# A recommender with cross layers on one core: weights laid out by the host, early rows of the first squares, and a later transpose of the second group

## Chip, cores and metric

One core of a Trainium2 chip runs the whole program. The metric is the device time of one execution in microseconds, the median of several runs. The profile shown is of one execution.

## The reference

39 embedding tables are looked up for a batch of 2048 rows, which gives `e` of (2048, 39, 16). Three cross layers follow (`w0` of 39x39x128, `w1` and `w2` of 39x64x128), then a sum over the 16 channels, the dense context, and three dense layers.

```python
x0 = xk = e                                             # (2048, 39, 16)
for idx, (W, b) in enumerate(((w0, b0), (w1, b1), (w2, b2))):
    z = relu(einsum('bhd,bkd,hks->bsd', x0, xk, W) + b[None, :, None])    # (2048, 128, 16)
    if idx < 2:
        xk = z[:, :64, :]; direct.append(z[:, 64:, :])
    else:
        direct.append(z)
z = sum(concatenate(direct, axis=1), axis=-1)           # (2048, 256)
h = concatenate([z, dense_ctx], axis=1)                 # (2048, 272)
h = maximum(h @ W_top1 + b_top1, 0); h = maximum(h @ W_top2 + b_top2, 0)
y = h @ W_top3
```

## The kernel before

**Groups, turns and tiles.** The batch is cut into 16 groups of 128 rows, and each group into two chunks of 8 channels, 1024 columns (`COLS`) each. A chunk is a turn, 32 in all (turn 0 to 31). A turn has 47 tiles: PAIRED, 0 to 19, cross layer 1 (each tile holds two fields h times 64 maps, 128 partitions); SQUARED, 20 to 26, cross layer 0 of the *next* chunk (three shifted copies of the 39 fields, 117 partitions; the last has 78); and LAST, 27 to 46, cross layer 2. Turn -1 has squares alone. Per tile VectorE multiplies two operands into a slot of `prod`, and TensorE contracts it over the partitions into PSUM (`zacc`). `PLAN` (line 58) gives each tile a letter: F tiles are contracted in float32 with `w_plain`; V, D and P tiles are split in a rounded `high` part (made by ScalarE) and a `low` part (VectorE for V and D, GpSimd for P), and contracted by three cheaper passes with `w_high` and `w_low`.

**Engines.** Each engine has its own stream, written by a function `emit(turn, j)` that `turns` calls for each turn and tile in order, the middle turns in a hardware loop. The streams meet in semaphores. An instruction that waits holds up everything behind it on its engine.

**Data.** x of a group is gathered by GpSimd (39 indirect DMAs into `landed`, line 602), transposed by TensorE in five blocks of 128 rows (the last has 112) into `maps2`, copied to `x` by ScalarE, and written twice in a row to DRAM (`x_periods`) by SP. From there SP loads `spread` (each field repeated over 64 partitions, two DMAs per piece of two tiles, ten pieces; line 510), `x_thrice` (three shifted copies of the 39 fields, line 500) and `shifted` (a ring of 4 slots, three DMAs of 39 rows of 4 KB per tile of squares, line 490). A slot of the ring is loaded again when the product that read it is done. In steady state the 20 spread loads of the next turn are issued during LAST, each after the product that frees its piece.

**The start.** Group 0 is gathered, turned and written block by block (`write_block`, line 521). w1 and w2 are loaded in four DMAs, and w0 in 50 short runs of a diagonal from SP and nearly as many from ScalarE's queue (lines 465 and 669), into space at the end of `spread`. ScalarE then copies tiles one by one into `w_plain`, `w_high` and PSUM (`cast_weights`), and VectorE subtracts for `w_low`. On SP, block q's write is followed, for q below 3, by a wait until it has landed and by the loads of two pieces of `spread`; blocks 3 and 4 follow without loads. Then `load_first` waits for all five blocks and loads x_thrice and four squares whole (`shifted` 0 to 3). The remaining four pieces of `spread` wait for the prepared weights (`s_prep`).

**The second group.** GpSimd copies its indices (`numbers`), issues 12 gathers at once, two per square of turn -1, and 13 in tiles 0 to 12 of turn 0. TensorE transposes it behind tile 13 of turn 0 (`TURN_AT`), ScalarE copies at 15, SP writes at 16, and from tile 20 (`GATHER_AT`) GpSimd gathers the next group.

**The end.** In turn 31 SP loads the top layers' weights and the dense context when tile 34's product is done (`load_top`, ten DMAs), ScalarE casts them behind tile 41, TensorE transposes the context in two halves (`turn_dense`, line 1073: behind tile 42 and after LAST), and VectorE makes the low parts of the first features and of the context (lines 972 and 965) after the last tile's low part. Then TensorE runs `MLP_STEPS`.

## Time and profile before

| | us |
|---|---|
| three timed runs, median (lowest to highest) | 2534.72 (2532.46 to 2537.24) |
| the profiled execution, its own time | 2519.62 |
| its span | 2517.8 |
| TensorE busy in the span | 2404.7 (96%) |
| VectorE busy | 2247.7 (89%) |
| GpSimd busy | 1687.2 (67%) |
| ScalarE busy | 1070.0 (42%) |
| mean granted clock of TensorE, share of full speed | 0.994 |

The span is the time between the first and last instruction of the profiled execution. Times in a timeline count from its start. The DMA share is the mean busy share of the core's 16 DMA engines; it can come out slightly over 1.

### The profile page before, as it was taken

What the parts mean: (1) busy time and instruction counts of PE and PEld (TensorE: products, weight loads), DVE (VectorE), ACT (ScalarE), POOL (GpSimd) and SP (SyncE); (2) the same over time, 40 slices, a digit from 0 to 9 for tenths busy, and PEclk for the clock granted to TensorE, in tenths of its full rate; (3) what the DMA queues carried; (4) which work ended last, traced back from release to release, by engine and by line L of the source; (5) the groups of instructions that cost most, each with busy time, mean ns of one, the idle gap of its engine ahead of it and who ended that gap; (6) DMA issues with size and microseconds to landing.
All of it is one profiled execution on the core that took longest, in us unless ns stands there. A gap on an engine that the chain in (4) does not pass through costs nothing.

```text
span 2517.8 us, 30358 instructions
## 1 busy us (share of the span) xinstructions
PE 2404.7 (96%) x7734; PEld 1447.4 (57%) x7734; DVE 2247.7 (89%) x1686; ACT 1070.0 (42%) x1124; POOL 1687.2 (67%) x1062
## 2 busy tenths in 40 slices
PE   0589999999999999999999999999999999999999
PEld 0355565555556665655566565556665565665556
DVE  0579999999999999999999999999999997999983
ACT  2234434444443444444344444444444443444445
POOL 6767676776767677776767677676768777544340
PEclk9999999999999999999999999999999999999999
DMA  7868889888888988888899888888998886998820
GB/s 151 189 142 192 193 194 213 197 191 199 192 198 194 221 195 195 199 190 200 191 207 205 195 197 193 200 191 197 217 198 201 191 199 159 211 203 194 188 70 11
DMA packets 184402, 469.77 MB, mean 187 GB/s; under 512 B 37842, under 2 KB 74307, under 8 KB 184371
## 3 DMA queue, kind: packets, MB, share of 16 engines
q1 hardware_dynamic: 161181, 461.92, 79.8%
q0 software_dynamic: 19968, 5.15, 2.0%
q10 hardware_dynamic: 3223, 2.35, 0.4%
q8 instruction: 13, 0.21, 0.0%
q14 instruction: 17, 0.14, 0.0%
HBM read 456.96 MB, written 12.33 MB: 186 GB/s over the span
## 4 chain that ended last, share of the span: by engine, by line
PE 73%; POOL 13%; issue 8%; DVE 2%; DMA 2%; SPq 2%; ACT 1%; POOLq 0%; DVEq 0%; ACTq 0%
PE zacc_a L1014 30%; PE zacc_b L1014 29%; POOL low L624 7%; POOL landed L602 6%; PE zacc_a L1049 5%; PE zacc_b L1049 5%; DMA x_periods<-x 1%; SPq L465 1%; DVE prod L908 1%; DMA shifted<-x_periods 1%; POOL mark L608 1%; PE zacc_a L1046 0%; PE zacc_b L1046 0%; ACT high L788 0%; PE maps L1056 0%
## 5 line engine op out<-in xcount | busy, mean ns | idle before, releaser
L624 POOL TENSOR_TENSOR low<-prod,high 128x1024 fp32r<-128x1024 f32 x384 | 945.8, 2472 | 579.8 <-ACT high L788 576.2
L908 DVE TENSOR_TENSOR prod<-spread,maps 128x2048 f32<-128x2048 f32 x448 | 1017.2, 2282 | 89.5 <-ACT direct L735 29.7
L788 ACT ACTIVATE high<-prod 128x1024 fp32r<-128x1024 f32 (+1 forms) x576 | 595.9, 1056 | 710.9 <-DVE prod L908 444.3
L602 POOL DMA_INDIRECT landed<-in_tbl,rows_id x624 | 672.4, 1078 | 179.2 <-issue 160.8
L1014 PE MATMUL zacc_a<-prod,w_plain 128*128 128x512 f32 (+2 forms) x1536 | 710.7, 597 | 30.0 <-DVE prod L893 24.1
L1014 PE MATMUL zacc_b<-prod,w_plain 128*128 128x512 f32 (+2 forms) x1536 | 705.3, 593 | 5.9 <-DVE prod L908 5.9
L1014 PEld LDWEIGHTS zacc_a<-prod,w_plain 128*128 128x128 f32 (+2 forms) x1536 | 292.5, 191 | 303.2 <-issue 271.2
L1014 PEld LDWEIGHTS zacc_b<-prod,w_plain 128*128 128x128 f32 (+2 forms) x1536 | 290.7, 189 | 274.3 <-issue 246.6
L893 DVE TENSOR_TENSOR prod<-shifted,x_thrice 117x1024 f32<-117x1024 f32 (+1 forms) x224 | 265.8, 1222 | 70.6 <-DMA shifted<-x_periods 53.3
L1049 PE MATMUL zacc_b<-low,w_high 128*128 128x512 f32 x672 | 280.4, 498 | 8.6 <-POOL low L624 8.6
L1049 PE MATMUL zacc_a<-low,w_high 128*128 128x512 f32 x672 | 280.3, 498 | 2.0 <-POOL low L624 2.0
L912 DVE TENSOR_TENSOR prod<-spread,maps 128x1024 f32<-128x1024 f32 (+1 forms) x224 | 265.6, 1210 | 0.0
L1014 PE MATMUL zacc_a<-high,w_low 128*128 128x512 f32 x672 | 239.0, 437 | 0.0
L1014 PE MATMUL zacc_b<-high,w_low 128*128 128x512 f32 x672 | 237.4, 434 | 1.5 <-ACT high L788 1.4
L1014 PE MATMUL zacc_a<-high,w_high 128*128 128x512 f32 x672 | 211.7, 396 | 0.0
L1014 PE MATMUL zacc_b<-high,w_high 128*128 128x512 f32 x672 | 211.3, 396 | 0.0
L1049 PEld LDWEIGHTS zacc_b<-low,w_high 128*128 128x128 f32 x672 | 126.8, 190 | 108.5 <-issue 82.8
L1049 PEld LDWEIGHTS zacc_a<-low,w_high 128*128 128x128 f32 x672 | 126.9, 189 | 101.3 <-issue 77.3
L865 DVE TENSOR_TENSOR low<-prod,high 128x1024 fp32r<-128x1024 f32 x128 | 165.0, 1289 | 0.0
L1014 PEld LDWEIGHTS zacc_b<-high,w_low 128*128 128x128 f32 x672 | 126.3, 189 | 58.3 <-issue 30.5
L1014 PEld LDWEIGHTS zacc_a<-high,w_low 128*128 128x128 f32 x672 | 126.1, 189 | 53.7 <-issue 30.7
L1014 PEld LDWEIGHTS zacc_a<-high,w_high 128*128 128x128 f32 x672 | 127.1, 189 | 29.9
(117 smaller groups left out, 1608.8 us busy)
## 6 DMA issues: line engine op xcount, KB each, us to landing
spread<-x_periods SPq DMA_DIRECT2D x608, 512.0 KB, 14.9
shifted<-x_periods SPq DMA_DIRECT2D x640, 156.0 KB
x_thrice<-x_periods SPq DMA_DIRECT2D x96, 156.0 KB
landed<-in_tbl,rows_id POOLq DMA_INDIRECT x624, 6.3
spread<-x_periods SPq DMA_DIRECT2D x32, 256.0 KB, 20.3
x_periods<-x SPq DMA_DIRECT2D x30, 256.0 KB, 3.6
spread<-features SPq DMA_DIRECT2D x4, 512.0 KB, 4.6
features<-feat ACTq DMA_DIRECT2D x15, 128.0 KB, 6.3
```

Of the source, the lines that this page charges most:

```text
L465: sp.dma_start(st0a[s * FIELDS + lo:s * FIELDS + hi, u, :], w0_run(f * FIELDS + g, hi - lo)).then_inc(s_wload, 16)
L602: nc.gpsimd.indirect_dma_start(out=landed[:, f, :], out_offset=None, in_=tables[f], in_offset=bass.IndirectOffsetOnAxis(ap=rows_id[:, f:f ...
L608: nc.gpsimd.tensor_tensor(mark[:, 0:1], mark[:, 0:1], mark[:, 1:2], ALU.add).then_inc(s_mark, 1)
L624: nc.gpsimd.tensor_tensor(low[0:rows, at_, :], prod[0:rows, at_, :], high[0:rows, slot(j, SPLIT, NH), :], ALU.subtract).then_inc(s_lowp, 1)
L788: nc.scalar.activation(high[0:rows, h, :], made(turn, j)[0:rows, :], ACT.Copy).then_inc(s_round, 1)
L865: nc.vector.tensor_tensor(to, whole, top, ALU.subtract).then_inc(s_lowv, 1)
L893: nc.vector.tensor_tensor(to, shifted[0:rows, u % RING0, :], x_thrice[0:rows, :], ALU.mult).then_inc(s_square, 1)
L908: nc.vector.tensor_tensor(prod[:, at_:at_ + 2, :], spread[:, t:t + 2, :], maps[:, :].unsqueeze(1).to_broadcast([128, 2, COLS]), ALU.mult). ...
L912: nc.vector.tensor_tensor(to, spread[0:rows, t, :], maps[0:rows, :], ALU.mult).then_inc(s_prod, 1)
L1014: return nc.tensor.matmul(z[:, hf * BANK:(hf + 1) * BANK], w, x[:, hf * BANK:(hf + 1) * BANK], start=start, stop=stop)
L1049: done = nc.tensor.matmul(z[:, cols], w_high[0:rows, r, :], x[:, cols], start=False, stop=last)
```

## The change

- The host lays out all weights (`laid_out`): w_plain and w_parted in the order of their slots, w0 as two tensors of 117 rows (`w0_ab`, `w0_ba`), biases and small vectors packed, the context already transposed (`dense_t`). They are loaded whole by SP: the plain tiles straight into `w_plain`, the parted ones into `prod`. ScalarE makes `w_high` in one instruction and VectorE sums the two halves of w0 and subtracts for `w_low`, one instruction each.
- SP, after block 3 has landed, loads the *early* rows (fields 0 to 31) of x_thrice and of squares 0 to 3; block 4 is then written, waited for, and the *late* rows (32 to 38) of x_thrice and square 0 are loaded from SP, those of squares 1 to 3 from ScalarE's queue.
- Group 1's gathers read `all_ids` directly, 20 ahead and one in each of tiles 0 to 18 of turn 0; each waits only for the transposes of the block it overwrites. Its transposes go behind tile 26 (into `maps1`), the copy to 27, the write to 28, and the third group's gathers begin behind tile 27.
- In turn 31 SP loads context and `W_top1`'s last rows at tile 0 into the free `shifted` and `x_thrice`; ScalarE casts them at tiles 6 to 16, GpSimd clears the gaps at tile 0, VectorE makes their low parts at tile 20. W_top1 and W_top2 are loaded behind tile 30's product and cast at tiles 36 and 39, the first features' casts move to tile 45, and their low part to tile 0 of turn 32. The context's transposes on TensorE are gone.

```diff
+TURN0_AT, COPY0_AT, WRITE0_AT, GATHER0_AT = 26, 27, 28, 27
+GATHERED_AHEAD = 20
-TOP_TILES, FEATS_TILES = 8, 12
-CAST_AT, TURN_TOP_AT = 41, 42
+TOP_TILES, FEATS_TILES, FH_TILES = 4, 8, 12
+CTX_AT = (6, 8, 12, 14, 16)
+CAST_AT, W1L_AT, FEATS_AT = (36, 39), 38, 45
...
+        def square_rows(u, late):
+
+            if late:
+                return [(FIRST_FIELDS - PER0 * u, FIELDS - PER0 * u)]
+            return [run for run in ((0, FIRST_FIELDS - PER0 * u), (FIELDS - PER0 * u, FIELDS)) if run[0] < run[1]]
+
+        def thrice_rows(s, late):
+
+            if late:
+                return [run for run in ((0, s), (FIRST_FIELDS + s, FIELDS)) if run[0] < run[1]]
+            return [(s, FIRST_FIELDS + s)]
+
+        FIRST_FIELDS = len(BLOCKS[0]) * (TURNED - 1)
...
+        def chunk0(first, rows):
+
+            flat = x_periods[0, :, :, :].rearrange("k (f d) b -> (k f) (d b)", d=DIM)
+            return flat[first:first + rows, 0:COLS]
+
+        def load_thrice0(engine, late):
+
+            for s in range(PER0):
+                for lo, hi in thrice_rows(s, late):
+                    engine.dma_start(x_thrice[s * FIELDS + lo:s * FIELDS + hi, :], chunk0(FIELDS - s + lo, hi - lo)
+                                     ).then_inc(s_thrice, 16)
+
+        def load_shifted0(engine, u, late):
+
+            for s in range(PER0):
+                for lo, hi in square_rows(u, late):
+                    engine.dma_start(shifted[s * FIELDS + lo:s * FIELDS + hi, u, :], chunk0(PER0 * u + lo, hi - lo)
+                                     ).then_inc(s_shifted[u], 16)
...
+            sp.dma_start(parts_in[:, 0:plan_r - PARTED0, :], a["w_parted"]).then_inc(s_parts, 16)
+            sp.dma_start(w_plain[0:TRIPLE, plan_f - PLAIN0:plan_f, :], a["w0_ab"][:, 0:PLAIN0, :]).then_inc(s_w0, 16)
+            sp.dma_start(w0_other, a["w0_ba"]).then_inc(s_w0, 16)
...
+            sp.dma_start(w_plain[:, 0:plan_f - PLAIN0, :], a["w_plain"]).then_inc(s_plain, 16)
+            sp.dma_start(bias[:, :], a["bias"]).then_inc(s_const, 16)
+            sp.dma_start(small[:, :], a["small"]).then_inc(s_const, 16)
...
-            third = -(-len(W0_RUNS) // EARLY_BLOCKS)
             for q in range(TURNED):
-                load_w0(W0_RUNS[third * q:third * (q + 1)])
                 write_block(q)
+                sp.wait_ge(s_first_w, 16 * PERIODS * (q + 1))
                 if q < EARLY_BLOCKS:
-                    sp.wait_ge(s_first_w, 16 * PERIODS * (q + 1))
                     for piece in (2 * q, 2 * q + 1):
                         load_spread(Turn(None, 0), piece)
+                elif q < TURNED - 1:
+                    load_thrice0(sp, 0)
+                    for u in range(RING0):
+                        load_shifted0(sp, u, 0)
+                else:
+                    load_thrice0(sp, 1)
+                    load_shifted0(sp, 0, 1)
+
+            def load_context():
+
+                sp.wait_ge(s_square, CHUNKS * N0)
+                sp.dma_start(m_dense, a["dense_t"]).then_inc(s_dense, 16)
+                sp.dma_start(m_w1d, a["w_top1d"]).then_inc(s_dense, 16)
...
                 if turn.fixed and turn.number() == CHUNKS - 1:
+                    if j == 0:
+                        load_context()
...
+            def cast_context(step):
+
+                if step == 0:
+                    act.wait_ge(s_dense, 32)
+                    act.wait_ge(s_gaps, 1)
+                if step < 4:
+                    at_, cols = 32 * (step % 2), slice(step // 2 * COLS, (step // 2 + 1) * COLS)
+                    nc.scalar.activation(m_ctx[at_:at_ + DENSE, cols], m_dense[:, cols], ACT.Copy).then_inc(s_dense_c, 1)
+                    return
...
-                if turn.fixed and turn.number() == CHUNKS - 1 and j == CAST_AT:
-                    cast_top()
-                if turn.fixed and turn.number() == CHUNKS and j == 0:
-                    high_features(0)
-                    copy_dense(0)
+                if turn.fixed and turn.number() == CHUNKS - 1:
+                    if j in CTX_AT:
+                        cast_context(CTX_AT.index(j))
+                    if j in CAST_AT:
+                        cast_top(CAST_AT.index(j))
+                    if j == FEATS_AT:
+                        high_features(0)
...
-                if turn.fixed and turn.number() == CHUNKS and j == SUB:
-                    split_top()
+                if turn.fixed and turn.number() == CHUNKS - 1 and j == SQUARED[0]:
+                    low_context()
+                if turn.fixed and turn.number() == CHUNKS and j == 0:
+                    low_features(0)
...
                 if turn.fixed and turn.number() == -1 and j == 0:
-                    pe.wait_ge(s_const, 16 * 4)
+                    pe.wait_ge(s_const, 16 * CONSTS)
                     turn_first()
...
-                if j == TURN_AT and not turn.odd and turn.shift(2).real():
+                if j == (TURN0_AT if turn.fixed and turn.number() == 0 else TURN_AT) and not turn.odd and turn.shift(2).real():
                     turn_x(turn.shift(2))
```

## Rows read from the trace of the kernel before

**Rows 1.** The page: busy time of each engine.

```profile
PE 2404.7 (96%) x7734; PEld 1447.4 (57%) x7734; DVE 2247.7 (89%) x1686; ACT 1070.0 (42%) x1124; POOL 1687.2 (67%) x1062
```

**Rows 2.** Stretches: length, each engine's busy time (instructions), PEclk, DMA share, GB/s.

```profile
103.00:145.60 42.60, 35.76 (x104) 21.50 (x104) 31.83 (x20) 11.89 (x13) 30.94 (x22) 0.86 0.47 126
145.60:217.95 72.35, 72.35 (x232) 43.41 (x231) 66.71 (x50) 31.29 (x30) 54.08 (x34) 1.00 0.82 184
```

**Rows 3.** Timeline of VectorE, the start (start us, us, what, idle before).

```profile
79.69 1.23 DVE L893 TENSOR_TENSOR prod<-shifted,x_thrice 117x1024 f32<-117x1024 f32 x1 [14.58 <-DMA shifted<-x_periods]
...
93.73 1.22 DVE L893 TENSOR_TENSOR prod<-shifted,x_thrice 78x1024 f32<-78x1024 f32 x1 [0.57 <-DMA shifted<-x_periods]
```

**Rows 4.** Timelines of TensorE and VectorE between LAST and the top layers.

```profile
2455.76 1.92 PE L1073 MATMUL maps<-spread 128*16 128x128 f32 x16
2459.31 0.47 PE L1134 MATMUL zacc_a<-spread_r 80*128 80x512 f32 x1 [1.63 <-issue]
...
2457.99 1.22 DVE L965 TENSOR_TENSOR spread_r<-maps,spread_r 16x1024 fp32r<-16x1024 f32 x1
```

**Rows 5.** Timeline of SP: loads issued.

```profile
58.27 2.58 SPq L510 DMA_DIRECT2D spread<-x_periods  x4
...
71.45 1.15 SPq L500 DMA_DIRECT2D x_thrice<-x_periods  x3
...
2351.50 28.97 SPq L510 DMA_DIRECT2D spread<-x_periods  x20
```

**Rows 6.** DMA issues at 58.3, 60.2, 61.3, 20.8 and 2380: KB, us to landing.

```profile
spread<-x_periods SPq DMA_DIRECT2D x1, 512.0 KB, 4.9
...
spread<-x_periods SPq DMA_DIRECT2D x2, 512.0 KB, 9.3
...
x_periods<-x SPq DMA_DIRECT2D x2, 64.0 KB, 9.2
...
x_periods<-x SPq DMA_DIRECT2D x1, 64.0 KB, 2.1
...
spread<-x_periods SPq DMA_DIRECT2D x1, 256.0 KB, 20.4
```

**Rows 7.** Stretches: spreads alone, 39-row loads, their last two engines, after w0 loads.

```profile
48.00:49.00 1.00, 0.00 (x0) 0.00 (x0) 0.00 (x0) 0.00 (x0) 0.85 (x1) 1.00 0.99 205
209.00:210.00 1.00, 1.00 (x6) 0.79 (x5) 1.00 (x1) 0.00 (x0) 0.69 (x2) 1.00 0.86 246
215.00:215.25 0.25, 0.25 (x2) 0.21 (x2) 0.25 (x1) 0.25 (x1) 0.25 (x1) 1.00 0.13 51
55.75:56.00 0.25, 0.00 (x0) 0.00 (x0) 0.00 (x0) 0.00 (x0) 0.00 (x0) 1.00 0.10 18
```

**Rows 8.** Timeline of TensorE, the transposes of x.

```profile
18.15 0.45 PE L1056 MATMUL maps<-ident,landed 128*128 128x128 f32 x1 [18.15 <-DMA landed<-in_tbl,rows_id]
...
39.90 0.48 PE L1056 MATMUL maps<-ident,landed 128*128 128x128 f32 x1 [12.88 <-DMA landed<-in_tbl,rows_id]
...
134.11 0.59 PE L1083 MATMUL maps<-ident 128*128 128x2 f32 x2 [4.80 <-DMA landed<-in_tbl,rows_id]
```

**Rows 9.** Timeline of GpSimd in turn 0.

```profile
122.67 0.95 POOL L602 DMA_INDIRECT landed<-in_tbl,rows_id  x1 [0.30 <-issue]
...
126.14 2.37 POOL L624 TENSOR_TENSOR low<-prod,high 128x1024 fp32r<-128x1024 f32 x1
128.68 1.77 POOL L602 DMA_INDIRECT landed<-in_tbl,rows_id  x1 [0.16 <-issue]
```

**Rows 10.** Turn 31: timelines of ScalarE and TensorE, then the chain, loop and LAST.

```profile
2390.93 1.06 ACT L788 ACTIVATE high<-prod 128x1024 fp32r<-128x1024 f32 x1 [1.32 <-DVE prod L908]
...
2394.02 0.62 PE L1014 MATMUL zacc_b<-high,w_low 128*128 128x512 f32 x2
...
2281.32 6.07 PE zacc_b L1014 x16
...
2420.44 8.91 PE zacc_b L1014 x16
```

More of the change, by code:

```diff
@@ L221, in build @@
         mark = sb("mark", [128, 2])
-        mark_dve = sb("mark_dve", [128, 2])
+        small = sb("small", [128, 8])
         rows_id = sb("rows_id", [ROWS, FIELDS], i32)
@@ L429, in build, with turned_in @@
-        early_tiles = [j for j in [*PAIRED, *LAST] if j not in later_split]
-        late_tiles = [*SQUARED, *later_split]
-        def weight_home(j):
-            tiles = early_tiles if j in early_tiles else late_tiles
-            r = [i for i in tiles if PLAN[i] != "F"].index(j)
-            return [*zacc, maps1][r // 8][:, r % 8 * MAPS:(r % 8 + 1) * MAPS]
+        def turned_in(n):
+            return maps1 if n.fixed and n.number() == 2 else maps2
         def first_bank(q):
             return q % 2 * BANK
-        def w0_run(start, n):
-            return w0.rearrange("h k s -> (h k) s")[start:start + (n - 1) * (FIELDS + 1) + 1:FIELDS + 1, :]
+        def square_rows(u, late):
+            if late:
+                return [(FIRST_FIELDS - PER0 * u, FIELDS - PER0 * u)]
+            return [run for run in ((0, FIRST_FIELDS - PER0 * u), (FIELDS - PER0 * u, FIELDS)) if run[0] < run[1]]
@@ L556, in emit @@
                 nxt, after = turn.shift(1), turn.shift(2)
-                if turn.fixed and turn.number() == -1 and j == 0:
-                    load_first(nxt)
-                if j == WRITE_AT and not turn.odd and after.real():
+                if j == (WRITE0_AT if turn.fixed and turn.number() == 0 else WRITE_AT) and not turn.odd and after.real():
                     write_x(after)
@@ L598, in _, with gather @@
             nc.gpsimd.memset(mark[:, :], 0.0).then_inc(s_mark, 1)
-            def gather(first, last, of=None):
+            def gather(first, last, of=None, rows=rows_id):
                 for f in range(first, last):
@@ L725, in take @@
                         act.wait_ge(s_sum01, turn.count(1, 1))
+                    if turn.fixed and turn.number() == 0:
+                        act.wait_ge(s_x, 2)
                     to, keep, s = maps1, HALF, s_z0
@@ L789, in emit @@
                                          ).then_inc(s_round, 1)
-                if j == COPY_AT and not turn.odd and turn.shift(2).real():
+                if j == (COPY0_AT if turn.fixed and turn.number() == 0 else COPY_AT) and not turn.odd and turn.shift(2).real():
                     copy_x(turn.shift(2))
@@ L1174, with laid_out, take, tile @@
-W0_RUNS = w0_runs()
-N_WLOADS = 2 * len(W0_RUNS) - sum(u == s == 0 for u, s, _, _ in W0_RUNS)
+def laid_out(given):
+    def take(name, dtype=np.float32):
+        return np.asarray(given.pop(name), dtype)
+    w0, flat = take("L0_rec_w0"), {1: take("L0_rec_w1").reshape(-1, MAPS), 2: take("L0_rec_w2").reshape(-1, MAPS)}
+    def tile(j):
+        t = j if j in PAIRED else j - LAST[0]
+        rows = flat[layer_of(j)][128 * t:128 * t + rows_of(j)]
+        return np.concatenate([rows, rows]) if stacked(j) else rows
+    ab, ba = np.zeros((TRIPLE, N0, MAPS), np.float32), np.zeros((TRIPLE, N0, MAPS), np.float32)
+    for n, j in enumerate(SQUARED_ORDER):
+        u, i = j - N1, np.arange(FIELDS)
+        for s in range(rows_of(j) // FIELDS):
+            f, g = (i - s) % FIELDS, (i + PER0 * u) % FIELDS
+            ab[s * FIELDS:(s + 1) * FIELDS, n] = w0[f, g]
+            if (u, s) != (0, 0):
+                ba[s * FIELDS:(s + 1) * FIELDS, n] = w0[g, f]
+    given["w0_ab"], given["w0_ba"] = ab, ba
+    for name, tiles in (("w_plain", PLAIN), ("w_parted", PARTED)):
+        given[name] = np.ascontiguousarray(np.stack([tile(j) for j in tiles if j not in SQUARED], axis=1))
+    given["bias"] = np.stack([take(b) for b in ("L0_rec_b0", "L0_rec_b1", "L0_rec_b2")], axis=1)
+    wt1, wt2 = take("W_top1"), take("W_top2")
+    given["w_top1"] = np.stack([np.concatenate([wt1[HALF:MAPS], wt1[:HALF]]), wt1[MAPS:2 * MAPS]], axis=1)
+    given["w_top1d"] = np.ascontiguousarray(wt1[2 * MAPS:])
+    given["w_top2"] = np.ascontiguousarray(wt2.reshape(4, 128, D3).transpose(1, 0, 2))
+    given["small"] = np.concatenate([take("W_top3").reshape(2, 128).T, take("b_top1").reshape(4, 128).T,
+                                     take("b_top2").reshape(2, 128).T], axis=1)
+    given["dense_t"] = np.ascontiguousarray(take("dense_ctx").T)
+    given["ident"] = np.eye(128, dtype=np.float32)
+    return given
```

304 lines of the change are left out of this document (120 added, 184 removed).

## The prediction

> **What bounds the kernel now.** I began with the page: TensorE is busy for 2404.7 of 2517.8 us and VectorE for 2247.7 [rows 1], so only time in which TensorE stands still, or does work that can go, can be won. Next, the stretches between one turn's squares and the next: inside the loop TensorE is busy for the whole of 72.35 us, at full clock [rows 2]. Nothing in the change touches that loop. What is open lies at the two ends, and I read those by the timelines of single engines. The first product of squares runs at 79.69 and the seventh at 93.73 [rows 3]; turn 0 then takes 42.60 us from its first PAIRED matmul (103.0) to the squares (145.6), with TensorE busy 35.76 of it and the clock granted at 0.86 [rows 2]. At the far end TensorE finishes LAST, transposes the context for 1.92 us, and starts the top layers at 2459.31 [rows 4]; from there it hardly pauses.
>
> **The start, step by step.** Today's chain on SP is: write a block of x, wait until it has landed, load four spreads; block 2's spreads are issued from 58.27 [rows 5]. One such step has a fixed length: of four spreads issued from 58.27 the first lands after 4.9 us and the last, issued at 60.2, after 9.3, at 69.5; the two writes issued behind them take 9.2 us although each has only 64 KB, where a write that follows nothing takes 2.1 [rows 6]. So transfers of one queue are served in order, and a write behind four spreads lands 12.2 us after the first spread's issue.
>
> The changed chain. The casts on ScalarE and the 50 narrow loads of w0 on each side go, but bias and small are now issued behind the weights, some 3.46 MB (23 parted and 17 plain tiles of 64 KB, twice 0.42 MB of squares), issued from 3.2 us. At about 220 GB/s, the rate of such stretches (205 and 246 in two of them [rows 7]), they are in near 21 us, and TensorE, which waits for all constants before its first transpose, starts near 21 instead of 18.15 [rows 8]. Copy and issue take 1 us, the write 2.1 alone and more behind the last weights: block 0 lands at about 25, with bounds at 23.5 and 27. Then 12.2 us to 37.2; block 2 is gathered only at 39.9 [rows 8], so its write goes out at 40.5 but lands behind the spreads at 49.5; 12.2 more, and block 3 has landed at 61.7. Now SP issues 24 loads of early rows, 15 times 128 KB. How they are dealt over the 16 DMA engines decides the case.
>
> What the rows show: 39-row loads keep the DMA share at 0.86 where spreads of 64 partitions keep 0.99, and yet move more, 246 against 205 GB/s [rows 7]. 0.86 is near 13 of 16, and 13 is the largest divisor of 39 up to 16. So I read: a transfer runs on as many engines as divide its rows. Early rows come in runs of 32, 26, 29, 23 and small ones; 29 and 23 have no divisor above 1, so all their rows go through one engine, 3 x 29 + 3 x 23 rows, and with its share of the others 183 rows of 4 KB, 750 KB, on the first engine, against 12 to 27 rows on the rest. Dealt evenly (3 rows per engine also gives 13 for 39) it would be 30. The trace has one hint more: the narrow loads of w0, runs such as 25, 23 and 21 rows, leave a tail in which 0.10 of the engines work, at 18 GB/s [rows 7]. I take the one-engine reading.
>
> The Trainium skill, DMA: Bandwidth & Descriptors, section Why a DMA increments its semaphore by 16 and not by 1, states that rule: the largest number up to 16 that divides the slowest dimension, the lowest engines first, 127 partitions all on one. The trace agrees for 39 rows, and no run here shows 29. By the rule the time is the forecast; by even dealing it would be the first rival's.
>
> Price: a lone engine. When two engines are left at work, 51 GB/s move [rows 7], 24.5 each, 0.17 us a row; in company 246/13 = 18.9, 0.22 us a row. 9 us in company take 41 rows, the other 142 take 24.2: 33.2 us, bounds 31 (all lone) and 40 (all in company), and 9 if dealt evenly. Block 4's write uses all engines and stands behind that: 61.7 + 2.6 + 33.2 + 1.1 = 98.6. Then 8 late loads on SP at 0.38 us (1.15 for three [rows 5]) and 2.1 to land: first product at 103.7, not 79.69. The first four then run back to back, the last three wait for their loads (each needs a slot that a product frees, some 4.7 us from there, 2.2 between two): the seventh ends 10.9 us after the first starts, at 114.6. Now it ends at 94.95 (93.73 [rows 3] and 1.22). **Cost +19.6 us** (+14 to +29); dealt evenly, 9 in place of 33.2 gives **-4**. Folding and splitting the weights, 7 and 23 tiles of 128 columns at the 1.23 us per 1024 of a product [rows 3], make 4.5 us on VectorE from 58 on, and the cast on ScalarE is earlier: all under this wait.
>
> **Turn 0.** TensorE no longer waits at tile 13 for the second group's gathers: 4.80 us now [rows 8], plus the transposes and a slow clock after it. What is late next is GpSimd: 20 gathers are ahead instead of 26, so six stand between its low parts of tiles 11 and 17, not two. Tile 11's ends at 128.5; the next gather comes at 128.68 and takes 1.77, a quiet one 0.95, with 0.30 before each [rows 9]. Two slow and four quiet ones reach 137.8, the low part of 2.4 us ends at 140.2, and the squares start at 140.7 instead of 145.6: **-4.9** (-6.4 to -2). The transposes come back behind tile 26, **+0.7**. SP's write of group 1 now waits for them, and turn 1's spreads, queued behind that wait on SP, start some 6 us later relative to the turn. The DMA share in turn 1 is 0.82 [rows 2], so it is mostly absorbed; **+1.0** (0 to 3). GpSimd's denser gathers of the third group fit in the idle time before its low parts; at one or two places within a us.
>
> **The end.** A new wait: in turn 31 SP issues the context loads at tile 0, when the last spreads have just been issued (2351.50 + 28.97 [rows 5]), and these take 20.4 us to land [rows 6]. The context is behind them in the same queue: in near 2402. ScalarE waits for it behind tile 6, with the casts of tile 7 and after queued behind. That cast runs at 2390.93 now, and TensorE takes tile 7 at 2394.02 [rows 10]. New: 2402.2, one context cast of 1.05, tile 7's of 1.06: 2404.3. TensorE stands for 10.3 us. After the pause before LAST its first 16 matmuls took 8.91 us where they take 6.07 in the loop [rows 10], so 2.8 more: **+13.1** (+10 to +15). VectorE's low_context (3 us at tile 20) then fits beneath. Casts of W1 and W2 move to tiles where ScalarE idles, with W1's low part on GpSimd.
>
> Against it: both context transposes go, 1.92 us each [rows 4], and what stands between LAST and the top layers: the context's low part and low_features, the last ending at 2459.2 [rows 4]. low_features now comes before tile 46's low part; that ends near 2452.7 and TensorE starts the top near 2454.0: **-5.3** (-6.5 to -4).
>
> **Sum**: 19.6 - 4.9 + 0.7 + 1.0 + 13.1 - 5.3 = +24.2 us, on the profiled execution's 2519.6 us (span and 1.8 around it), that is 2543.8 there. The three timed runs have a median of 2534.7, 15.1 above the profiled one; both ends are unlikely to change that, so 2534.7 + 24.2 = 2558.9.
>
> **The rivals.** First, early rows dealt evenly, the rest as above: +24.2 - 23.6 = +0.6, 2535.3, no change. For: 3 rows on 13 engines fits 0.86 too; against: the tail of few engines. 0.14. Second, a faster outcome: even dealing, and the context is not behind the spreads (small rows overtaking): 13.1 becomes 0.7 for low_context in a gap that it does not quite fit, so 2534.7 - 11.8 = 2522.9; against: the 64 KB write that took 9.2 us. 0.07. Third, one engine for the early rows, but no wait for the context: 2546.5. 0.12. Fourth, worse: turn 1's DMA backlog does not drain and the early loads go at 18.9 GB/s: 2570. 0.07. It decides from a backlog of about 6 us on, the slack between the last spread's landing and its product.
>
> **Numbers.** The forecast has 0.60. Its own range is 2550 to 2568. With the third rival inside, 0.72 is held; reaching to the first takes it to 0.86, so 2533 to 2568. One case in a few will be off in its own size. Faster or slower by 0.2% is 5.1 us, about what a measurement of this kernel tells from nothing: faster 0.09 (the second and part of the first), same 0.13, slower 0.78.
>
> **What would show it.** In the new profile: one SP stretch of 24 loads near 62 us followed by 20 to 30 us with a DMA share near 0.06 and about 24 GB/s; first product of squares near 104; no wait of TensorE on gathers at tile 13, a short one on GpSimd near tile 19; in turn 31 a wait of about 10 us on ScalarE's cast at tile 7; top layers starting at once behind LAST. If the share stays near 0.9 after the early loads and the first product comes near 80, the dealing was even and the forecast is wrong by 24 us; if tile 7 is not late, the order of the queue was misread, and 12 us go.

## The result and the profile after

The changed kernel takes 2553.0 us (median of 4 runs, 2551.7 to 2558.0) beside 2534.9 for the kernel before on the same chip: ratio 1.0075, 95% interval 1.0062 to 1.0087, 18 us slower. The forecast was 2559, with a range of 2533 to 2568 and 0.78 for slower. The number came near, but the sum behind it did not hold as written: one term was absent on this chip, and others that I had not seen or had put too low stood in its place.

One fact is needed to read any of it. The kernel before does not take the same time on all chips: 2535.7 and 2535.5 us on two chips of the experiments, 2516.4 and 2518.2 on two others. Its shown profile (2519.6) is of the quick kind, the times of the study of the slow kind. This is the start of the kernel before on a chip where it takes 2516, SP's timeline (start us, us, what) and VectorE's first and seventh product of squares:

```profile
15.74 5.74 SPq L465 DMA_DIRECT2D spread<-in_L_rec_w  x17
...
28.99 6.87 SPq L465 DMA_DIRECT2D spread<-in_L_rec_w  x17
...
79.45 1.22 DVE L893 TENSOR_TENSOR prod<-shifted,x_thrice 117x1024 f32<-117x1024 f32 x1 [13.44 <-DMA shifted<-x_periods]
...
93.57 1.22 DVE L893 TENSOR_TENSOR prod<-shifted,x_thrice 78x1024 f32<-78x1024 f32 x1 [0.72 <-DMA shifted<-x_periods]
```

And the same kernel where it takes 2535:

```profile
15.84 13.94 SPq L465 DMA_DIRECT2D spread<-in_L_rec_w  x17
...
39.94 18.23 SPq L465 DMA_DIRECT2D spread<-in_L_rec_w  x17
...
98.63 1.22 DVE L893 TENSOR_TENSOR prod<-shifted,x_thrice 117x1024 f32<-117x1024 f32 x1 [14.77 <-issue]
...
112.81 1.22 DVE L893 TENSOR_TENSOR prod<-shifted,x_thrice 78x1024 f32<-78x1024 f32 x1 [0.98 <-DMA shifted<-x_periods]
```

Seventeen narrow loads of w0 take SP 5.74 us on one chip and 13.94 on the other, the next seventeen 6.87 and 18.23. On the slow kind nearly all of SP's issues stand 0.70, 1.40 or 2.1 us apart between 18 and 58 us, where those of w0 stand 0.3 to 0.4 apart on the quick kind. I call SP *stepped* there. It steps once more from 92 to 108 us, beside the second group's gathers:

```profile
91.27 17.58 SPq L490 DMA_DIRECT2D shifted<-x_periods  x20
```

These 20 loads take 12.33 us on the quick kind. That costs the start nothing: from the first to the seventh product are 14.1 us on the quick chip and 14.2 on the slow one. The changed kernel was profiled on a chip of the slow kind, and it steps too, in another place. Its SP timeline, one issue alone, and VectorE's first and seventh product:

```profile
59.81 1.27 SPq L464 DMA_DIRECT2D x_thrice<-x_periods  x3
61.12 27.56 SPq L471 DMA_DIRECT2D shifted<-x_periods  x21
88.68 0.70 SPq L542 DMA_DIRECT2D x_periods<-x  x2
...
76.08 0.70 SPq L471 DMA_DIRECT2D shifted<-x_periods  x1
...
99.11 4.63 DVE L896 TENSOR_TENSOR prod<-shifted,x_thrice 117x1024 f32<-117x1024 f32 x4 [36.09 <-DMA shifted<-x_periods]
...
109.14 1.22 DVE L896 TENSOR_TENSOR prod<-shifted,x_thrice 78x1024 f32<-78x1024 f32 x1 [1.13 <-DMA shifted<-x_periods]
```

And two stretches of it (length, busy time of PE, PEld, DVE, ACT and POOL, PEclk, DMA share, GB/s):

```profile
64.00:72.00 8.00, 0.00 (x0) 0.00 (x0) 0.00 (x0) 0.00 (x0) 6.02 (x7) 1.00 0.22 48
...
84.00:92.00 8.00, 0.00 (x0) 0.00 (x0) 0.00 (x0) 0.00 (x0) 0.00 (x0) 1.00 0.14 46
```

The 21 early loads of squares take 27.56 us to issue while the DMA engines are used at a share of 0.22, then 0.14: up to 89.4 it is SP that binds, not the engines. Behind that, block 4's write takes until 93.9 to land.

Turn 0 and turn 1, TensorE: the first PAIRED matmuls of turn 0, the squares of turn 0 and of turn 1, and the two long waits:

```profile
120.42 3.75 PE L1011 MATMUL zacc_a<-prod,w_plain 128*128 128x512 f32 x4 [5.86 <-DVE prod L911]
...
159.16 1.22 PE L1046 MATMUL zacc_a<-low,w_high 128*128 128x512 f32 x2 [4.50 <-POOL low L643]
160.18 6.13 PE L1011 MATMUL zacc_b<-prod,w_plain 117*128 117x512 f32 x8
...
218.57 1.22 PE L1046 MATMUL zacc_b<-low,w_high 128*128 128x512 f32 x2 [6.23 <-DVE low L866]
...
244.91 3.60 PE L1011 MATMUL zacc_a<-prod,w_plain 117*128 117x512 f32 x8
```

[rows 2] has 103.0, 145.6 and 217.95 for the three. Turn 0 is 39.76 us in place of 42.60 (43.4 in the two other traces of the kernel before). The 4.80 us on the gathers [rows 8] are gone and 4.50 on GpSimd's low part of tile 17 have come; behind that wait the squares begin at half clock, the 1.2 GHz level (granted 0.56 of full speed from 160.2 to 166.0; eight matmuls in 6.13 us, 3.60 at full clock). Turn 1 is 84.73 us in place of 72.35 [rows 2]. Its long wait is on a low part of VectorE:

```profile
207.15 1.22 DVE L866 TENSOR_TENSOR high<-prod,high 64x1024 fp32r<-64x1024 f32 x1
...
210.60 7.92 DVE L866 TENSOR_TENSOR low<-prod,high 128x1024 fp32r<-128x1024 f32 x1
...
204.82 0.96 POOL L621 DMA_INDIRECT landed<-in_tbl,rows_id  x1 [0.16 <-issue]
...
207.34 1.85 POOL L621 DMA_INDIRECT landed<-in_tbl,rows_id  x1 [0.31 <-issue]
209.49 0.95 POOL L621 DMA_INDIRECT landed<-in_tbl,rows_id  x1 [0.30 <-issue]
210.46 6.96 POOL L643 TENSOR_TENSOR low<-prod,high 128x1024 fp32r<-128x1024 f32 x3
```

A subtraction of as many columns (on 64 partitions) takes 1.22 us at 207.15, the one at 210.60 takes 7.92, and over that time GpSimd runs three low parts with nothing between them, from 210.46 to 217.42.

The end: SP's loads, then ScalarE and TensorE in turn 31, the first matmuls of LAST (2460.53), and the first of the top layers:

```profile
2379.14 28.61 SPq L531 DMA_DIRECT2D spread<-x_periods  x20
2407.80 0.59 SPq L561 DMA_DIRECT2D shifted<-in_dense_t  x1
...
2429.95 1.06 ACT L764 ACTIVATE shifted_r<-shifted 16x1024 fp32r<-16x1024 f32 x1 [13.35 <-DMA x_thrice<-in_w_top1d]
...
2432.00 1.22 PE L1011 MATMUL zacc_b<-high,w_low 128*128 128x512 f32 x2 [10.84 <-ACT high L798]
...
2460.53 3.75 PE L1011 MATMUL zacc_b<-prod,w_plain 128*128 128x512 f32 x4 [5.89 <-DVE prod L911]
...
2495.15 0.73 PE L1043 MATMUL zacc_b<-high,w_low 128*128 128x512 f32 x2 [1.55 <-DVE high L866]
...
2496.19 0.40 PE L1121 MATMUL zacc_a<-shifted_r,x_thrice_r 80*128 80x512 f32 x1
...
2497.13 0.63 PE L1125 MATMUL zacc_a<-spread_r 128*128 128x512 f32 x1
```

The context loads leave SP behind the last 20 spreads and land 21 us after their issue; ScalarE stands 13.35 us and TensorE 10.84, close to the 10.3 forecast.

Put against a trace of the kernel before on the same kind of chip, stretch by stretch (us; a turn from the first matmul of PAIRED to the squares, or from squares to squares):

| | before, quick chip | before, slow chip | after (slow chip) | after less before, slow |
|---|---|---|---|---|
| start, to the first PAIRED matmul | 102.86 | 122.10 | 120.42 | -1.7 |
| turn 0, to its squares | 43.37 | 43.45 | 39.76 | -3.7 |
| to turn 1's squares | 72.31 | 72.34 | 84.73 | +12.4 |
| rest | 2298.3 | 2298.2 | 2311.3 | +13.1 |
| span | 2516.8 | 2536.1 | 2556.2 | +20.1 |

The profiled execution of the changed kernel is 5 us above its other three; the medians differ by 18. The two columns of before differ in the start alone. The rest, +13.1, is not all at the end: +1.7 lies in turns 2 to 30 (1.5 of it from the squares of turn 3 to those of turn 4, 77.36 us in place of 75.85; its cause is open), and +11.35 from turn 30's squares (2367.72, before 2359.00) to the end.

### The profile page after: what moved, and what is told of

It is laid out like the page before. It is cut to its first block, busy times and chain, and to the rows that moved or that the text cites. A ratio compares the mean times of both kernels' runs of the same rounds, so it can differ in the third digit from the quotient of the medians.

```text
span 2556.2 us, 30130 instructions
## 1 busy us (share of the span) xinstructions
PE 2407.8 (94%) x7702; PEld 1448.5 (57%) x7702; DVE 2251.4 (88%) x1657; ACT 1058.5 (41%) x1053; POOL 1689.2 (66%) x1059
## 3 DMA queue, kind: packets, MB, share of 16 engines
HBM read 457.02 MB, written 12.33 MB: 184 GB/s over the span
## 4 chain that ended last, share of the span: by engine, by line
PE 67%; POOL 12%; issue 8%; DVE 3%; DMA 1%; ACT 0%; POOLq 0%; SPq 0%; ACTq 0%; DVEq 0%
PE zacc_a L1011 28%; PE zacc_b L1011 26%; POOL low L643 6%; POOL landed L621 5%; PE zacc_a L1046 5%; PE zacc_b L1046 5%; DMA x_thrice<-in_w_top1d 1%; DVE prod L911 1%; DVE low L866 1%; POOL mark L627 1%; PE zacc_b L1043 0%; PE zacc_a L1043 0%; DVE zacc_a L915 0%; DVE prod L915 0%; PE maps L1053 0%
## 5 line engine op out<-in xcount | busy, mean ns | idle before, releaser
L621 POOL DMA_INDIRECT landed<-in_tbl,rows_id x585 | 631.3, 1079 | 166.4 <-issue 150.8
L866 DVE TENSOR_TENSOR low<-prod,high 128x1024 fp32r<-128x1024 f32 x128 | 171.7, 1341 | 0.0
L1011 PEld LDWEIGHTS zacc_b<-high,w_high 128*128 128x128 f32 x672 | 127.8, 190 | 30.1
```

The source lines that it names most:

```text
L621: nc.gpsimd.indirect_dma_start(out=landed[:, f, :], out_offset=None, in_=tables[f], in_offset=bass.IndirectOffsetOnAxis(ap=rows[:, f:f + 1 ...
L866: nc.vector.tensor_tensor(to, whole, top, ALU.subtract).then_inc(s_lowv, 1)
L1011: return nc.tensor.matmul(z[:, hf * BANK:(hf + 1) * BANK], w, x[:, hf * BANK:(hf + 1) * BANK], start=start, stop=stop)
```

## The experiments

All ratios are to the kernel before on the same chip; what its time there was is said, since it tells the kind of chip.

**e1_even: the early rows dealt evenly.**

```diff
-            return [run for run in ((0, FIRST_FIELDS - PER0 * u), (FIELDS - PER0 * u, FIELDS)) if run[0] < run[1]]
+            n = FIRST_FIELDS - PER0 * u
+            cuts = (0, n) if n in (32, 26) else (0, 16, n) if n == 29 else (0, 13, n)
+            return [*zip(cuts, cuts[1:]), *([(FIELDS - PER0 * u, FIELDS)] if u else [])]
```

> The changed kernel with the early rows of squares 1 and 3 cut differently: 29 rows as 16 + 13, 23 rows as 13 + 10, the same rows to the same places, 6 loads more. One-engine reading: the most loaded DMA engine then carries some 33 rows in place of 183; the 27.56 us of issuing shrink to about 9, the last block has landed near 77 instead of 93.9, the first product of squares comes near 83 instead of 99.1, and the time falls by 15 us (12 to 18), to 1.001 of the kernel before. Rival, that the loads were slow beside the second group's gathers, however they are dealt: the issuing stays at 27 us or more, first product at 99 or later, ratio 1.0075 or a little above.

Measured: ratio 1.0065 (1.0052 to 1.0079), before 2535.7. The expected 15 us did not come; the first product is at 98.2. SP's timeline:

```profile
61.48 29.23 SPq L473 DMA_DIRECT2D shifted<-x_periods  x27
90.76 0.80 SPq L544 DMA_DIRECT2D x_periods<-x  x2
92.83 1.49 SPq L466 DMA_DIRECT2D x_thrice<-x_periods  x5
```

27 loads take 29.23 us, again stepped: cutting a load in two gives the engines less each and SP more to issue. What did change is the tail. Block 4's write leaves SP at 90.8 to 91.6 and has landed at 92.8; in the changed kernel it leaves at 88.7 and lands at 93.9, at a DMA share near one engine in 16. So the write lands 5.2 us after it leaves SP with the uneven dealing and 2.0 with the even one: the uneven dealing is there, but most of it is hidden by SP on this chip. The median, 2553.2 beside 2553.0, does not move, and the test does not tell what the dealing costs where SP does not step.

**e2_ctx: the context loads ahead of the last spreads.**

```diff
-                    if j == 0:
-                        load_context()
+                if turn.fixed and turn.number() == CHUNKS - 2 and j == LAST[0]:
+                    load_context()
```

> The changed kernel with the two context loads issued one turn earlier, ahead of the last turn's spreads instead of behind them. Queue reading: the 10.8 us in which TensorE stood for ScalarE's cast of tile 7 in turn 31 go, and the slow clock behind them (about 2 us): 10 to 13 us less than the changed kernel, ratio 1.0025. Cost bounded at 1 us: the spreads leave SP a little later. Rival, that the loads are slow by themselves or that something else holds ScalarE there: the wait stays, ratio 1.0075.

Measured: ratio 1.0026 (1.0017 to 1.0035), before 2535.7: 12.4 us less than 1.0075, as expected. The loads, from the DMA issues around them (KB each, median us to landing):

```profile
shifted<-in_dense_t SPq DMA_DIRECT2D x1, 128.0 KB, 2.7
```

TensorE at the end, timeline:

```profile
2448.92 3.75 PE L1011 MATMUL zacc_b<-prod,w_plain 128*128 128x512 f32 x4 [5.89 <-DVE prod L911]
...
2483.51 0.73 PE L1043 MATMUL zacc_b<-high,w_low 128*128 128x512 f32 x2 [1.54 <-DVE high L866]
...
2484.54 0.40 PE L1121 MATMUL zacc_a<-shifted_r,x_thrice_r 80*128 80x512 f32 x1
```

Issued first they land in 2.7 us, and TensorE's 10.84 us wait is gone: their place behind the spreads in the queue was the cause. LAST to top layers is 35.62 us (2448.92 to 2484.54), 35.66 in the changed kernel (2460.53 to 2496.19); before it was 38.87 [rows 4, 10]. Here the top layers run at full clock from their first matmul.

**e4_whole: no early rows; block 4 is written at once, then 15 whole loads.**

```diff
-                elif q < TURNED - 1:
-                    load_thrice0(sp, 0)
-                    for u in range(RING0):
-                        load_shifted0(sp, u, 0)
-                else:
-                    load_thrice0(sp, 1)
-                    load_shifted0(sp, 0, 1)
+                elif q == TURNED - 1:
+                    load_first(Turn(None, 0))
```

(and the late loads on ScalarE's queue go)

> The changed kernel without early rows: block 4 is written as soon as it is copied, and then the 15 whole loads of 39 rows are issued as in the kernel before. If the early rows only stood in the way: block 4 is issued near 60, has landed near 62.5, and as in the kernel before 8.2 us lie between the first of these loads and the first product of squares, so near 71 in place of 99.1, 28 us earlier. GpSimd still has 20 gathers to issue and may give 5 of it back in turn 0. 23 to 28 us less than the changed kernel, ratio 0.9965 (0.995 to 0.9985). Rival, that the DMA engines are held by the gathers in this stretch so that whole loads are slow too: first product near 90 or later, ratio 1.004 or more.

Measured: ratio 0.9998 (0.9986 to 1.0011), before 2535.7. That is some 19 us less than the changed kernel, and less than the 23 to 28 expected. So on this kind of chip the early rows cost 19 us over not having them. The first product is where I put it, the seventh is not:

```profile
63.20 3.50 SPq L520 DMA_DIRECT2D x_thrice<-x_periods  x3
67.40 23.13 SPq L510 DMA_DIRECT2D shifted<-x_periods  x20
...
70.13 1.23 DVE L887 TENSOR_TENSOR prod<-shifted,x_thrice 117x1024 f32<-117x1024 f32 x1 [6.93 <-DMA shifted<-x_periods]
...
93.32 1.22 DVE L887 TENSOR_TENSOR prod<-shifted,x_thrice 78x1024 f32<-78x1024 f32 x1 [1.17 <-DMA shifted<-x_periods]
```

20 loads of 39 rows take 23.13 us here, 13.75 in the shown trace of the kernel before (SP's timeline, from 72.64), and PAIRED starts at 102.61. Whole loads step as early ones do, and until about the same time.

**e5_old2: the second group at its old places.**

```diff
-TURN0_AT, COPY0_AT, WRITE0_AT, GATHER0_AT = 26, 27, 28, 27
-GATHERED_AHEAD = 20
+TURN0_AT, COPY0_AT, WRITE0_AT, GATHER0_AT = 13, 15, 16, 20
+GATHERED_AHEAD = 26
```

(and the group's transposes into `maps2`, as before)

> The changed kernel with the second group back at its old places: 26 gathers ahead, turned behind tile 13, the third group's gathers from tile 20. Theory: turn 0 gets its wait of some 4.8 us at tile 13 back (+3), and turn 1 loses its 6 us wait behind tile 46's neighbours, the slow clock after it and the transposes (84.7 back to about 74): 7 to 9 us less than the changed kernel in all, ratio 1.0042. Rival, that turn 1 is late from the DMA work that the slow start pushed into it: turn 1 stays near 84, turn 0 gets 3 longer, ratio 1.0085.

Measured: ratio 1.0045 (1.0031 to 1.0058), before 2535.7: 7.6 us less. PAIRED starts at 121.93, squares at 164.06 and 236.37: turn 0 gives back 2.4 us and turn 1 is 72.31 again, 12.4 less. The placement of the second and third groups' work was the whole of turn 1's loss. The 7.6 us here and the 12.4 of e2_ctx make 20.0, as much as the whole loss; the two edits were not run together with the early rows.

**e9_calm: no gathers just before GpSimd's three low parts in a row.**

```diff
-def gather_slots(behind):
+def gather_slots(behind, none=()):
...
-    free = [p for p in range(behind + 1, 2 * TILES) if PLAN[p % TILES] != "P"]
+    free = [p for p in range(behind + 1, 2 * TILES) if PLAN[p % TILES] != "P" and p not in none]
...
-GATHERS, GATHERS0 = gather_slots(GATHER_AT), gather_slots(GATHER0_AT)
+GATHERS, GATHERS0 = gather_slots(GATHER_AT), gather_slots(GATHER0_AT, range(44, 53))
```

> The changed kernel, but none of the third group's gathers stands at places 44 to 52, before and among GpSimd's three low parts in a row at the start of turn 1 (tiles 3, 4, 5); they are spread over the other places. Theory: these gathers made GpSimd late, its three low parts ran back to back, and VectorE's low part beside them took 7.92 instead of 1.22 us; without them VectorE's takes 1.2 to 3 us, TensorE's wait of 6.2 us and the slow clock behind it go, turn 1 takes 84 instead of 92.2 from first product to first product: 7 to 9 us less than the changed kernel, ratio 1.0043. Rival: turn 1 is late because the group is turned behind tile 26 and its spreads come later; then the 92.2 stay, ratio 1.0075.

Measured: ratio 1.0128 (1.0111 to 1.0145), but before takes 2516.4 here, so the ratio does not stand beside 1.0075; the trace does:

```profile
209.72 1.22 DVE L866 TENSOR_TENSOR low<-prod,high 128x1024 fp32r<-128x1024 f32 x1
...
207.40 2.41 POOL L643 TENSOR_TENSOR low<-prod,high 128x1024 fp32r<-128x1024 f32 x1 [2.05 <-ACT high L798]
211.88 4.75 POOL L643 TENSOR_TENSOR low<-prod,high 128x1024 fp32r<-128x1024 f32 x2 [2.07 <-ACT high L798]
```

VectorE's low part takes 1.22 us, TensorE's wait of 6.2 us is gone, and turn 1 is 75.72 us (squares at 160.57 and 236.29) instead of 84.73: 9.0 us. The group is still turned behind tile 26. So most of turn 1's loss comes from where the third group's gathers stand. The other 3.4 us were not taken apart; the transposes and a half clock behind turn 0's wait (eight matmuls in 4.90 us) lie in them.

By the whole time the gain is smaller. Turn 2 takes 76.40 us here and 74.64 in the changed kernel, so 1.8 of the 9.0 come back. The median is 2549.3 us (2545.9 to 2551.6), 3.7 below the changed kernel's 2553.0 on another chip, where 7 to 9 were expected. The cleaner pair is e11_even and e1_even, which differ by this edit alone and ran on chips of one kind: 2547.1 beside 2553.2, 6.1 us.

This trace also shows the start on a chip where SP does not step, SP's timeline and two stretches:

```profile
60.80 18.77 SPq L471 DMA_DIRECT2D shifted<-x_periods  x21
79.62 1.25 SPq L542 DMA_DIRECT2D x_periods<-x  x2
93.26 1.49 SPq L464 DMA_DIRECT2D x_thrice<-x_periods  x5
```

```profile
72.00:80.00 8.00, 0.00 (x0) 0.00 (x0) 0.00 (x0) 0.00 (x0) 5.97 (x7) 1.00 0.16 35
84.00:92.00 8.00, 0.00 (x0) 0.00 (x0) 0.00 (x0) 0.00 (x0) 0.00 (x0) 1.00 0.06 26
```

SP has issued all 24 early loads and the write behind them by 80.9 (five of the loads take it 1.2 to 3.8 us each). The gathers end at 82.3. From 84 to 92 nothing else is under way and the share is 0.06 at 26 GB/s, one engine of 16, until block 4 lands at 93.3. This is the stretch that I had forecast (a share near 0.06 and about 24 GB/s), though it stands alone for 9 us and not for the 20 to 30 forecast. PAIRED starts at 120.94, against 102.86 for the kernel before on this chip: +18.1.

**e11_even: e9 with even early rows.** The edit is that of e1_even on top of e9_calm.

> The version without gathers at places 44 to 52, with the early rows of squares 1 and 3 dealt as 16 + 13 and 13 + 10. Where SP issues at its normal pace nothing hides the one engine: that version then had its first product at 98.8 and a stretch of one engine in 16 (share 0.06, 25 to 27 GB/s) up to 92. One-engine reading: with even pieces block 4 is written near 72, the first product comes near 82, and the time is 14 to 17 us less, ratio 1.007 in place of 1.0128. Rival: early rows are slow for another reason, first product near 98 again, ratio 1.013. If SP is in its slow state on this chip, first product near 98 in any case, ratio 1.004.

Measured: ratio 1.0045 (1.0031 to 1.0059), before 2535.5: SP stepped again (27 loads in 29.18 us, first product at 97.8), the case that the expectation names last. So no run has even pieces on a chip where SP does not step, and what the dealing costs there is untested.

**e6_before and e12_before: the kernel before again.**

> The kernel before, unchanged, for a second trace of it. Its timed runs lie 15 us above the one profiled execution shown. In every trace of the changed kernel and its variants so far SP runs at one instruction in 0.70 us from about 61 to 89 us, while GpSimd issues gathers; the shown trace of the kernel before has no such stretch. If this state is usual and the shown trace a rare one without it, this trace shows the 0.70 us steps too, the seventh product of squares near 108 in place of 93.7, and a time near 2535. Rival: the state belongs to the changed kernel alone; then this trace has SP at 0.41 us a load, the seventh product near 94, and the 15 us lie elsewhere.

> The kernel before once more, to see whether its time of 2516 or 2535 goes with SP's state. If its time is near 2535 here, its trace has to show steps of 0.70 us on SP between 72 and 90 and a seventh product of squares near 108 or a start of turn 0 some 15 us later than 103.0; if it is near 2517, none of this. Rival: a time near 2535 with an undisturbed start; then the 18 us between chips lie elsewhere.

Measured: 2518.6 us without steps beside runs of 2516.4, and 2537.9 with them beside 2535.5. My first guess, that the steps are the usual case and the shown trace a rare one, is wrong as put: they go with the chip. The second expectation holds in the main: with the longer time come the steps and a seventh product at 112.8. But the steps that cost the time lie between 18 and 58 us, in the loads of w0; those from 92 to 108 are there as well, and cost nothing.

**e7_hold and e8_act: gathers held back, and the loads on another engine**, both on top of e4_whole.

```diff
                     pool.wait_ge(s_all, 16)
+                    pool.wait_ge(s_square, 4)
```

> The changed kernel without early rows (15 whole loads behind block 4), and GpSimd issues the second group's 20 gathers only once four products of squares are made. Theory: SP's slow state comes from gathers being issued at the same time; without them the 15 loads take 0.4 us each again, first product near 70, seventh near 84 instead of 93.3, turn 0 some 8 us earlier, 6 to 10 us less than the version with whole loads alone: ratio 0.9965. The gathers then run to about 105 and may push GpSimd's low parts of turn 0 by 2 to 4 us. Rival: the state has another cause (time since the start, instruction loading); then the steps of 0.70 us stay until about 89 and the seventh product comes near 93 as before, ratio 1.000 to 1.002.

```diff
-                elif q == TURNED - 1:
-                    load_first(Turn(None, 0))
...
+            act.wait_ge(s_first_w, 16 * PERIODS * TURNED)
+            for s in range(PER0):
+                act.dma_start(x_thrice[s * FIELDS:(s + 1) * FIELDS, :], flat0[FIELDS - s:2 * FIELDS - s, 0:COLS]
+                              ).then_inc(s_thrice, 16)
```

(and the 12 loads of squares likewise)

> The changed kernel without early rows, the 15 whole loads issued by ScalarE, idle then, instead of SP; the gathers are as in the changed kernel. If the slow state is SP's own, ScalarE issues the 15 loads at 0.3 to 0.4 us each and they land at 200 GB/s and more: seventh product near 85 instead of 93.3 if SP's later nine loads are not slow too, ratio 0.997 to 0.999. If everything that issues transfers beside the gathers is slow, ScalarE's loads are 1.2 to 1.4 us apart as SP's are, seventh product near 93, ratio 1.000.

Measured, before 2516.4 for both: 1.0080 (1.0067 to 1.0093) and 1.0031 (1.0019 to 1.0042). On this chip SP does not step in any trace, so neither tells what stops the steps; that part failed. What they tell is where GpSimd binds. With the gathers held, PAIRED starts at 91.30 (102.61 in e4_whole), but TensorE then waits for GpSimd, which is still at its gathers:

```profile
110.01 1.22 PE L1038 MATMUL zacc_a<-low,w_high 128*128 128x512 f32 x2 [8.11 <-POOL low L637]
```

Turn 0 takes 51.9 us (91.30 to 143.22; 39.7 in e4_whole, to 142.33), and more than the earlier start is given back. With ScalarE issuing, PAIRED starts at 94.63 and turn 0 takes 39.44 us (to 134.07), and only turn 1 (83.04) and the end remain of the losses. Both ratios are above what was expected (0.9965, and 0.997 to 0.999).

**e10_best and e13_behind26: combinations.** Both are e8_act with e2_ctx; e10 has the second group as e5_old2, e13 as e9_calm.

> A combination: no early rows, the 15 whole loads issued by ScalarE behind block 4, the second group turned behind tile 13 with 26 gathers ahead as in the kernel before, the context loads issued ahead of the last spreads. From the parts: the version with whole loads from ScalarE was 8.7 us slower than the kernel before on its chip; less 8 to 10 us in turn 1 and less 9 to 10 at the end gives 0.9960 of the kernel before (0.9945 to 0.9975) where SP issues at its normal pace. Where SP is in its slow state the kernel before takes 2535 instead of 2516 and this one hardly changes, as only nine small groups of loads are SP's then: ratio 0.990. If the second group's gathers hold turn 0 up again (they end no earlier, while the squares come 8 us earlier), 5 us of it are lost: 0.998.

> The combination again, but with the second group as in the changed kernel (20 gathers ahead, turned behind tile 26) and no gathers at places 44 to 52: whole loads from ScalarE, context loads ahead of the last spreads. In the last combination turn 0 took 63.9 us from first product to first product, 10 of it because ScalarE stood until 99.1 (6 us behind the last gather), and 4.7 because TensorE waited for gathers at tile 13. With six gathers fewer ahead both go: first product near 70, turn 0 in 54 to 56, turn 1 in 82.5 to 84.5, so 6 to 9 us less than the last combination: 2509, ratio 0.989 (0.987 to 0.991) beside a kernel before of 2535, or 0.9955 (0.994 to 0.997) beside one of 2516. Rival: on an early start GpSimd's gathers bind wherever the group is turned, then the time is that of the last combination, 0.9923 or 1.000.

Measured: e10 2516.7 us, ratio 0.9923 (0.9910 to 0.9937), before 2535.5, where 0.990 was expected for that kind of chip. e13 2507.0 us, ratio 0.9959 (0.9945 to 0.9973), before 2518.2, at the 0.9955 expected for that kind of chip. Both are faster than the kernel before on the chip where they ran; the changed kernel did not run beside them, but was slower than before where it did. In e10, ScalarE's timeline on a chip where SP steps:

```profile
62.39 1.41 ACTq L706 DMA_DIRECT2D x_thrice<-x_periods  x3
63.83 5.03 ACTq L710 DMA_DIRECT2D shifted<-x_periods  x12
99.14 1.07 ACT L738 ACTIVATE maps<-zacc_a,bias 64x1024 f32<-64x1024 f32 x1 [39.49 <-remote]
```

ScalarE issues 15 loads in 6.5 us, unstepped, where SP took 21 (63.20 to 84.2 in e4_whole). But its next instruction, whose input TensorE had ready at 88.3, starts at 99.1, 6 us after the last gather (issued at 92.23 for 0.94). So e10's PAIRED starts at 105.06, e13's at 94.11, on a chip without steps. How e13 does where SP steps was not tried.

## Why the prediction came out right, and where it did not

**The start, +19.6.** Right where SP does not step: +18.1 (e9_calm against e6_before), by the mechanism named, one engine left at work at 26 GB/s. The number is helped by a second error, though. Block 4 has landed at 93.3, not 98.6, the first product runs at 98.8, not 103.7, and the seventh ends at 110.1, not 114.6, 15.3 us later than before. The other 2.8 are TensorE's, a term put at nothing: the seven products come so close together that it finishes its squares 4.8 us behind the last of them, 2.0 before. Wrong on the chips of the timed runs: -1.7. The step that failed is the one ahead of it, that the chain of the kernel before in the shown trace (block, spreads, block) is its chain in the timed runs as well. I had noted that these runs lie 15 us above the profiled one and wrote that "both ends are unlikely to change that". The 15 us were in the very stretch that the change replaces: there the narrow loads of w0 held SP until 58 us. With them gone the changed kernel does not pay that; it pays for its early rows instead, and starts at nearly the same time. Dealing them evenly gains nothing as long as SP binds. The divisor rule that I took from the Trainium skill, DMA: Bandwidth & Descriptors, section Why a DMA increments its semaphore by 16 and not by 1, is in keeping with e9's stretch of one engine, and with the write that lands 2.0 us after its issue in e1_even and 5.2 in the changed kernel; no run shows what even dealing gains where SP does not step.

**Turn 0, -4.9 and +0.7.** -3.7 in all (-4.2 forecast). The wait moved where it was put, GpSimd's low part of tile 17, and that ended 38.7 us after the first PAIRED matmul in place of 37.2: four of the six gathers before it took 1.4 to 2.0 us, not two. Against the trace that the forecast was worked from (42.60) the change is -2.8.

**Turn 1, +1.0 for a backlog of transfers.** This is the large miss: +12.4. Of GpSimd's denser gathers I had written that they "fit in the idle time before its low parts; at one or two places within a us". I had added up their time but not asked what stands next to them: four gathers ahead of tiles 3, 4 and 5 make GpSimd late, its three low parts run as one block of 6.96 us, and VectorE's low part beside it takes 7.92 us instead of 1.22. e5_old2 (72.31) and e9_calm (75.72) show it from two sides. The term that was in the sum, a backlog of transfers, is not what was lost: e9_calm keeps the late transposes and spreads and is 3.4 us above the 72.31 in all. That VectorE and GpSimd hold each other up through a shared path is my reading; the runs show the slow instruction, and that it is gone when the block is broken up.

**The end, +13.1 and -5.3.** +11.35 from turn 30's squares to the end, +7.8 forecast. The wait was right: 10.84 us beside 10.3, and with the slow clock behind it the stretch up to LAST grew by 13.1 (92.81 us, before 79.72), to the tenth what was forecast; e2_ctx takes 12.4 off. The gain was too large. LAST to top layers fell by 3.2 us, not 5.3, because tile 46's low part now runs beside a low part of W2 on GpSimd and takes 3.27 us, so that TensorE waits 1.55. And in the changed kernel the first top matmuls ran at half clock, the 1.2 GHz level (granted 0.51 from 2496.5 to 2499.7), 1.5 us more (2496.19 to the end is 60.0 us, 58.5 before), a price that was not in the sum. Why they do so here and not in e2_ctx, where TensorE waits as long just before, is open.

**The sum.** 19.6 - 4.2 + 1.0 + 7.8 = +24.2 was forecast, -1.7 - 3.7 + 12.4 + 13.1 = +20.1 is what the two traces show. The start was too high by 21 us; turn 1 was too low by 11, the end by 3.5, turn 0 by 0.5, and the 1.7 in turns 2 to 30 had no term. That the number is right is luck: the forecast has errors of opposite sign that nearly cancel, and none of the four rivals is what happened.

## What to carry to other kernels

When a profiled execution and the timed runs differ by more than the runs among themselves, find out in which stretch before adding terms: if it lies in the stretch that the change rewrites, the sum does not carry over. Give a load a number of rows that many engines divide, but count the issues too, as more loads can cost what the even dealing gains. Short transfers that someone waits for go ahead of the long ones in a queue, or on another engine's queue. And when work is packed into an engine's idle time, look at which of its longer instructions then run back to back, and who works beside them.

## What the hardware showed that I had not expected

- On two of the four chips of the experiments (and on that of the changed kernel's profile) SP issues in steps of 0.70 us for a stretch of the start. The stretch ends 3 to 7 us after GpSimd's last gather in a row: gathers end at 51.5, 105.5, 82.6 and 84.9, the steps at 58.2, 108.1, 89.4 and 89.8 (kernel before twice, changed kernel, e4_whole). ScalarE's stall until 99.1 in e10_best ends likewise, 6 us after 93.2. What makes it is open: the same gathers stand beside an unstepped SP on the other chips, and in the slow trace of the kernel before they stand beside SP's first issues too, up to 18 us, which are not stepped.
- A VectorE subtraction of 128 x 1024 took 7.92 us in place of 1.22 beside three GpSimd low parts without a gap. It began 0.14 us after the first of them and ended 1.1 us after the third. One GpSimd low part can do it too: in the changed kernel the subtraction at 2469.89 took 3.39 us and tile 46's 3.27, each ending 1.1 us after the GpSimd instruction that ran when it began. Most of the others start beside no GpSimd low part, or late in one, and take 1.22 to 1.3.
- The 128 KB load of the context landed in 2.7 us when issued ahead of 20 spreads; issued behind them, at 2407.8, it landed after 21 us and held ScalarE until 2429.95.
